# Two heads with both kinds of attention in one item, row tiles in pairs, and normalisation after attention

## The reference

```
q, k, v = heads(x @ qkv_w + qkv_b)
std_logits = (q . k) / 4                              # "dot", 16 numbers a head
write = exterior(x_prev @ w1_write, x @ w2_write)     # 6 numbers a head, unit length
read  = exterior(x @ w1_read,  x @ w2_read)
geo_logits = (read . (write @ J6)) * inc_scale        # "geometric", 6 numbers a head
std_out = softmax(causal(std_logits)) @ v
geo_out = softmax(causal(geo_logits)) @ (x @ geo_w + geo_b)
gate = mean over heads of sigmoid(x @ gate_w + gate_b)
x = layernorm(x + ((1-gate)*std_out + gate*geo_out) @ out_w + out_b)
x = layernorm(x + (silu(x @ wg.T) * (x @ wu.T)) @ wd.T)    # 768 hidden columns
```

## Time and profile before

| | us |
|---|---|
| median of 3 runs | 2109.17 (2107.64 to 2111.22) |
| the profiled execution, span | 2112.1 |
| PE busy | 1930.6 (91%) |
| ACT busy | 1273.4 (60%) |
| DVE busy | 1129.4 (53%) |
| POOL busy | 336.9 (16%) |

### The profile page before, as it was taken

One profiled execution on the slowest core, in us unless ns is written; L12 is line 12 of the kernel. 1 busy time (PEld: TensorE's weight loads), 2 busy tenths in 40 slices (PEclk: granted clock), 3 DMA queues, 4 the chain that ended last, 5 costly groups with the idle time before them and its releaser, 6 DMA issues. The chain is left out here.

```text
span 2112.1 us, 35917 instructions
## 1 busy us (share of the span) xinstructions
PE 1930.6 (91%) x11400; PEld 769.0 (36%) x11400; DVE 1129.4 (53%) x2179; ACT 1273.4 (60%) x1641; POOL 336.9 (16%) x609
## 2 busy tenths in 40 slices
PE   8888498999998999999899999989999995899998
PEld 4444122333332333333233333323333322556555
DVE  5666377565564655556465655646565403443442
ACT  4555544577776777677677767767777783222121
POOL 3333303111211110111111011111101111000000
PEclk9999699999999999999999999999999997999999
DMA  6668660404133250414324041432500004112000
GB/s 192 205 211 254 163 107 25 86 21 90 37 70 46 50 86 6 91 20 73 49 47 86 6 91 21 72 46 50 86 6 30 4 11 103 43 51 65 20 20 20
DMA packets 138525, 145.83 MB, mean 69 GB/s; under 512 B 46784, under 2 KB 120768, under 8 KB 136288
## 3 DMA queue, kind: packets, MB, share of 16 engines
q1 hardware_dynamic: 137136, 140.32, 30.4%
q0 software_dynamic: 624, 2.75, 0.4%
q10 hardware_dynamic: 576, 0.28, 0.1%
HBM read 88.25 MB, written 54.53 MB: 68 GB/s over the span
## 5 line engine op out<-in xcount | busy, mean ns | idle before, releaser
L931 ACT ACTIVATE prob<-ex 128x1024 f32<-128x1024 f32 (+2 forms) x1280 | 1074.5, 893 | 444.4 <-PE ex L776 438.8
L946 DVE TENSOR_REDUCE mp<-mx 128x1 f32<-128x512 f32 (+3 forms) x1280 | 749.2, 609 | 547.4 <-PE mx L794 287.5
L776 PE MATMUL ex<-qa,ka 98*128 98x512 bf16 (+3 forms) x2560 | 675.6, 354 | 62.7 <-issue 28.3
L827 PE MATMUL pv<-prob,va 128*32 128x512 f32 (+3 forms) x5120 | 613.4, 552 | 7.6 <-POOL prob L752 7.3
L791 PE MATMUL mx<-ka,qa 96*128 96x512 bf16 (+3 forms) x1280 | 450.1, 353 | 14.7 <-DVE mp L946 13.8
L752 POOL TENSOR_SCALAR_AFFINE_SELECT prob<-prob 128x256 f32<-128x256 f32 x512 | 205.8, 408 | 1288.3 <-ACT prob L931 1287.8
L776 PEld LDWEIGHTS ex<-qa,ka 98*128 98x128 bf16 x2560 | 200.2, 99 | 474.3 <-ACT prob L931 306.3
L791 PEld LDWEIGHTS mx<-ka,qa 96*128 96x128 bf16 x1280 | 123.7, 97 | 340.4 <-DVE mp L946 239.1
L827 PEld LDWEIGHTS pv<-prob,va 128*32 128x32 f32 x5120 | 101.7, 108 | 206.7 <-issue 181.8
L1291 ACT ACTIVATE sg<-pg 128x512 f32<-128x512 f32 x48 | 28.7, 597 | 185.6 <-PE pg L1213 185.5
L794 PE MATMUL mx<-mask_qk,ident 128*128 128x128 bf16 x512 | 113.1, 221 | 0.0
(11 more groups left out here) (101 smaller groups left out, 964.7 us busy)
## 6 DMA issues: line engine op xcount, KB each, us to landing
parts<-sp SPq DMA_DIRECT2D x64, 384.0 KB, 3.3
qa<-parts SPq DMA_DIRECT2D x192, 128.0 KB, 6.7
ka<-parts SPq DMA_DIRECT2D x192, 128.0 KB, 8.6
values<-vn SPq DMA_DIRECT2D x64, 256.0 KB, 3.3
va<-values SPq DMA_DIRECT2D x16, 1024.0 KB, 13.8
heads<-on SPq DMA_DIRECT2D x64, 128.0 KB, 1.9
att<-heads SPq DMA_DIRECT2D x64, 128.0 KB, 3.0
xc<-in_xt SPq DMA_DIRECT2D x8, 513.0 KB, 4.2
```

Source lines behind the costliest of these rows:

```text
L776: last = pe.matmul(dst, ka[which][0:NROWM, h, kb * P:(kb + 1) * P], qa[which][0:NROWM, h, (qt + 1) * CH - w:(qt + 1) * CH], start=True, st ...
L827: last = pe.matmul(pv[h * VW:(h + 1) * VW, qt % 2, CH - w:CH], va[kind][:, kb, h * VW:(h + 1) * VW], prob[(s * HG + h) % 8][:, at[j]:at[j] ...
L931: act.activation(prob[n % 8][:, 0:w], ex[:, n % 2, 0:w], ACT.Exp).then_inc(ex_done, 1)
L946: v.tensor_reduce(out=mp[kind][:, h * NKB + qb, k0 // CH:k0 // CH + 1], in_=mx[:, u % 2, 0:w], axis=AX.X, op=ALU.max).then_inc(mx_free[kin ...
```

## The change

An item now holds two heads with both kinds (16 items again, each a batch and a pair of heads). Four streams are in it: geometric and dot of head 0 and head 1.

- Scores: the geometric ones of the two heads stand in rows 0 to 37 and 64 to 101 of one operand, as two row tiles of 64x128 (six products of 6 rows and two rows for the maxima). The dot ones take 98 rows for the first head and 128 for the second, one after the other. One exponential covers one kind of both heads and one key block of 512 or 384 columns.
- Maxima of the dot scores come in pairs of row tiles too (`max_pair`, K = 64: four of the six products), into a ring of three banks. The mask is added by DVE while it reduces. All items have them, 80 tiles for the next item; 80 stand in a prologue ahead of item 0. The branch over the geometric maxima stands in every item.
- The V product has its four column tiles for the four streams, one bank, and stands between the geometric and the dot scores of a key block. V is padded with ones, so the denominators come out on 16 rows. `turn` and the division go; the products are stored as they are (`raw`).
- Row maxima are written by eight DMAs an item instead of two. There are three operand sets, loaded two items ahead.
- `project` makes six packed rows a chunk instead of eight: the lines have 6 numbers a head and no padding.
- `finish` loads values and denominators (9 DMAs, 2.5 MB a chunk), DVE inverts the denominators (`inverse`), POOL multiplies (`weigh`, four operations), DVE adds the two kinds (`mixed`). The transposes of the mix go, as the stored products already stand turned. The gates are worked out in the last item of attention.

```diff
-HG = 4
+PAIRS_OF_HEADS = H // 2
+ITEMS = B * PAIRS_OF_HEADS
+MX_RING = 3
...
+                        if kind == GEO:
+                            rows = slice(HALF * a, HALF * a + GEO_FULL)
+                            lhs, rhs = k_set[rows, kb * P:(kb + 1) * P], q_set[rows, (qt + 1) * CH - w:(qt + 1) * CH]
+                        else:
+                            rows = slice(0, DOT_FULL[a])
...
+            def max_pair(nxt, u):
...
+                for a in range(2):
+                    t = 2 * u + a
+                    if t >= MX_RING:
+
+                        pe.wait_ge(mx_free, nit * NTILE + t + 1 - MX_RING)
+                    rows = slice(HALF * a, HALF * a + DOT_MAIN)
+                    pe.matmul(mx[:, t % MX_RING, 0:w], q_set[rows, a, qb * P:(qb + 1) * P],
+                              k_set[rows, a, k0:k0 + w], start=True, stop=True).then_inc(mx_ready, 1)
...
+                for j in range(groups):
+                    scores(it, which, s, j, GEO, head)
+                    some(j)
+                    earlier(j)
+                    scores(it, which, s, j, DOT, head)
+                    if j == groups - 1:
+                        some(groups)
+                    if j == 0 and s == MT_STEP and nxt:
+                        max_rows(nxt)
...
+                for a in range(2):
+                    for i in range(2):
...
+                            q.dma_start(dst.rearrange("p (k t) -> p k t", t=P),
+                                        mrow[n:n + NKB, i, :]).then_inc(m_in, 16)
...
+            def inverse(c, par):
+
+                v.wait_ge(att_in[par], (c // 2 + 1) * 9 * 16)
+                v.sem_inc(v_passed, 1)
+                v.reciprocal(den[par][:, :, :, :], den[par][:, :, :, :]).then_inc(inv_ready, 1)
...
                     if m == 2 and has_mix:
-                        mixed(c + 2, par, False)
+                        inverse(c + 2, par)
...
+                if has_mix:
+                    mixed(c + 2, par, False)
                 add_up(c, par, SECOND, not has_second)
```

More of the change, by code:

```diff
@@ new lines, in step, with earlier @@
+            def step(at, before, nxt, s, head):
+                it, which, use = at
+                places = shares(s) if nxt else [[] for _ in range(1 + len(STEPS[s][1]))]
+                groups = len(STEPS[s][1])
+                def some(i):
+                    for u in places[i]:
+                        max_pair(nxt, u)
+                def earlier(j):
+                    prev, ps = (at, s - 1) if s else (before, NSTEP - 1)
+                    if prev is not None and j < len(STEPS[ps][1]):
+                        times_v(*prev, ps, j, head)
+                for j in range(groups):
[7 more added lines that the diff above has]
+                        max_rows(nxt)
+                for j in range(groups, 2):
+                    earlier(j)
@@ new lines, in item @@
+            def item(at, before, nxt, head):
+                it, which, use = at
+                pe.wait_ge(sets[which]["geo_in"], (use + 1) * LOADS * 16)
+                pe.wait_ge(m_in, (it + 1) * 128)
+                for s in range(NSTEP):
+                    step(at, before, nxt, s, head)
+                    if s == 3 and isinstance(it, int) and it == LAST_ITEM:
+                        pe.wait_ge(gate_ready, 4)
+                        pe.transpose(mx[0:NC * TT, 0, 0:P], gate[:, :], ident[:, :]).then_inc(gate_turned, 1)
@@ L921, in _ @@
+            for it in range(ITEMS - 3, ITEMS):
+                item(static(it), static(it - 1), static(it + 1) if it < LAST_ITEM else None, False)
+            times_v(*static(LAST_ITEM), NSTEP - 1, 0, False)
         @block.scalar
@@ L1026, in _, with finish @@
+            for u in range(NMT):
+                max_pair(0, u)
+            max_rows(0, True)
+            item(0, True, True)
+            with v.Fori(1, ITEMS - 1) as it:
+                item(it, False, True)
+            item(ITEMS - 1, False, False)
             take(ITEMS - 1, NQT - 1, False)
-            normalise(ITEMS - 1, NQT - 1, False)
-def finish(nc, x, heads, gate_z, ident, weights, out):
+def finish(nc, x, raw, gates, ident, weights, out):
     NT = NC * TT
@@ L1438, with by_pair @@
     qkv_w, qkv_b = a["attn_qkv_w"], a["attn_qkv_b"]
+    def by_pair(geo, dot):
+        both = [v.reshape(v.shape[:-1] + (PAIRS_OF_HEADS, 2 * DH)) for v in (geo, dot)]
+        return np.stack(both, -2).reshape(geo.shape[:-1] + (2 * D,))
     laid = {
```

971 lines of the change are left out of this document (492 added, 479 removed).

## The result

| | before | forecast | after |
|---|---|---|---|
| median of the runs, us | 2109.08 (2107.64 to 2111.22) | 2036 | 2489.96 (2486.89 to 2496.95) |
| span of the profiled execution, us | 2112.1 | 2039 | 2485.2 |
| first scores at, us | 250.71 | 288 | 340.17 |
| end of attention at, us | 1763.4 | 1586 | 2027.66 |
| output layers, us | 348.7 | 453 | 457.5 |

The changed kernel is slower: ratio 1.181 (95% interval 1.179 to 1.183). The forecast missed the sign, and the time lies outside the range. Of the 446.2 us by which the span misses the forecast, 52.2 come from the start (340.17 against 288), 389.5 from attention (1687.5 against 1298), 4.5 from the output layers.

A forecast was written before the change was run, and what follows sets the result against it. PE was taken to set attention's pace. Attention ending at 1586 (first scores 288, 15 items of 82, a last of 66) plus output layers 453 gave 2039, on the runs' scale 2036 us, 3.5% faster; range 1945 to 2165.

The forecast's parts named there:

- the end of an item: Attention, between items: PE waits about 3 us for eight row DMAs; with branch and clock 7.2 (5.3 to 8.1); nothing else late.
- rival of a lower clock in attention: Attention: gaps every few us lower the granted clock, 0.97 before; over 2150 us, chance 0.04.
- The start: Projections 25 us shorter (10 to 40), then memsets 11.5, prologue 49, rows 10: first scores at 288 against 250.71.
- PE's stream: PE in attention: row tiles run at once, third tile-shape change 0.09 each; 70.5 us an item.
- rival of pairs one by one: Attention on PE: row tiles don't run at once, 14.8 us more an item, 2265 us; chance 0.14.
- part case of 0.28 a pair: Attention on PE: row-tile pairs at 0.28 in place of 0.22 us, adding 69, 2105 us; chance 0.06.
- The masked reduction: DVE in attention: adding the mask while reducing costs the plain 0.61 us, over 32 of 80 tiles an item.
- rival of a doubled price: DVE in attention: masked reduction at twice the price, prologue 14 us longer, PE waiting 5 more an item: 2125; chance 0.13.
- The item: Attention: 70.5 stream, 3.5 ring, 7.2 end of item, 0.6 bank exchange make 82 us an item (77 to 90).
- the ring: Attention: three banks of maxima make PE wait about one tile's 0.5 us in seven steps, 3.5 an item.
- The skipped branch: Ends of items: the branch over exact geometric maxima, now in every item, idles PE 0.75 to 2.3 us.
- The output layers: Head 25 us more, six rounds 13.5 more each (10.6; 16.6 if DVE and POOL take turns), transposes 2 less: 453.

The follow-up runs named there:

- e1: The changed kernel with each operand load issued as two DMAs, one a slot, rows outermost: 2198.65 us, 1.043 to the kernel before.
- e4: The changed kernel with four buffers instead of two for the V products on their way out, nothing else: 2182.98 us, 1.035 to the kernel before.
- e5: The changed kernel with loads by rows, stores as two DMAs of 64 rows, and four output buffers together: 2136.71 us, 1.015 to the kernel before.
- e6: e5 with the transpose of the maxima and the eight row DMAs one step earlier: 2131.82 us, 1.012 to the kernel before.
- e7: e5 with a chunk's reciprocal in six pieces, the mix behind the third sum, POOL's products started per kind: 2077.63 us, 0.985 to the kernel before.

## Why the prediction was wrong, step by step

**The step that failed** is the sentence on the end of an item: the eight row DMAs stand on SP ahead of the 24 loads and the store, and "those have a whole item until needed (three operand sets), so nothing else is late". That holds for the loads, not for the store: its buffer is one of two, and DVE's next copy but one needs it. It put the delay at nothing. What the runs showed in its place is a wait of some 22 us in 13 of the items, 291.4 us of DVE, and 298.0 of PE behind it. And the loads got no price at all, though the diff turns their outermost dimension from 16 rows to 2 slots. No row of before shows a load of the new shape, and the sentence gave it neither a lower nor an upper bound. With rows outermost in the loads (e1) or the wait taken out (e4) 291 and 307 us of the miss go, and with both and the store by rows (e5) 351 of the span. None of the rivals named this: they looked at PE and DVE, and the DMA queue was treated as an order without a rate. The rival of a lower clock in attention names what went with the stall: 0.87 in the kernel after is 0.95 in e5.

**The start.** A chunk's chain on DVE did get shorter, 22.6 us from one to the next (101.02 to 123.65) in place of 27.36, more than the 3.0 charged. What the sum left out is SP's queue here too. Operands are now loaded two items ahead, so the 24 loads of the second item stand in the projections, and they are slow. First, ACT waits 30.7 us in all for stores that stand among the loads of the first item, so its last operation there ends only 2.8 earlier than before (233.1 against 235.9). Second, the last chunk's stores stand behind the 24 loads of the second item, which are issued from 219.06 on:

```profile
252.74 12.62 SPq L337 DMA_DIRECT2D parts_dot<-sp  x4
```

Attention begins when they have landed; until then ACT is idle for 41.2 us (the line of ACT L982 above), where it was 5.8 before. So attention's first operation on ACT came 32.7 us later than before in place of 25 earlier. In e5 ACT's last operation ends 24.1 earlier than before, as forecast, though as a larger gain less 9.2 of such waits; but it is idle for 18.2 behind it, since the loads stand ahead of the last stores there too, and attention starts 11.7 earlier. That lies near the lower bound of 10, by luck: the bound was set for ACT and the gates, not for SP. Memsets took 11.9 (11.5 charged). The prologue to the transpose took 46.4 (286.24 to 332.64; charged 49), and the rows 7.5 (charged 10).

**PE's stream.** The row tiles do run at once, and this term was right. PE in mid-item, kernel after, answers to the earlier trace rows:

```profile
1041.48 1.06 PE L902 MATMUL pv<-prob,va 128*32 128x512 f32 x8
1042.48 0.61 PE L836 MATMUL ex<-dq,dk 98*128 98x512 bf16 x2
1043.07 0.39 PE L836 MATMUL ex<-gq,gk 38*128 38x512 bf16 x2
1043.30 0.38 PE L857 MATMUL mx<-dk,dq 64*128 64x512 bf16 x2
1043.61 1.06 PE L902 MATMUL pv<-prob,va 128*32 128x512 f32 x8
1044.61 0.61 PE L836 MATMUL ex<-dq,dk 98*128 98x512 bf16 x2
1045.15 0.39 PE L836 MATMUL ex<-gq,gk 38*128 38x512 bf16 x2
```

A pair of 512 columns starts 0.23 before what follows (1043.07 to 1043.30), as a single whole-array matmul did. Two dot matmuls take 0.54 to 0.59 until the next pair, 0.44 by themselves: 0.10 to 0.15 for the third change of tile shape (charged 0.09). From one V block to the next it is 2.13 (1041.48 to 1043.61), as forecast (2.1). The rival of pairs one by one, and the part case of 0.28 a pair, fell.

**The masked reduction** has the plain price. The groups by line, kernel after (busy us, mean ns, idle before):

```profile
L1010 DVE TENSOR_REDUCE mp<-mx 128x1 f32<-128x512 f32 x768 | 490.7, 685 | 294.2 <-PE mx L857 294.0
L1006 DVE CUSTOM_DVE_ANT_0 dull<-mx,mask_qk 128x128 f32<-128x128 f32 (+3 forms) x512 | 234.1, 489 | 304.6 <-PE mx L857 300.6 <-issue 3.3
...
L1006 DVE DVE_READ_ACCUMULATOR2_ANT mp<- 128x1 f32 x512 | 42.7, 83 | 0.0
```

And one of 512 columns in order of time:

```profile
1003.38 0.69 DVE L1006 CUSTOM_DVE_ANT_0 dull<-mx,mask_qk 128x512 f32<-128x512 f32 x1
```

It takes 0.69 where the plain one takes 0.64 to 0.65, with 0.08 behind it for the result; the rival of a doubled price fell.

**The item.** In the kernel after the first and the last of fifteen items, without the wait for the store, take 86.5 us, the others 109 to 113.6. In e5 they take 84.1 to 89.1, mean 87.0, against 82 (77 to 90): right in kind, 5 short. In the one e5 item at full clock (984.29 to 1068.43, 84.1) PE is busy 73.9 where 70.5 were counted. The waits in e5's fifteen items, prologue left out, are 3.0 each for ACT's exponentials (45.4; charged 0.6), 3.1 for the rows (37.1, and 8.7 at three ends of items that the view names issue and that are gone in e6; charged 3) and 1.3 for the ring (19.3; charged 3.5). With 73.9 that is 81.3; the rest of the 84.1 is in smaller waits, 0.9 of it for POOL's masks. The other 3 of the 87 go with the clock (0.94 in an item of e5 from 816 to 900 us, 1.00 in the one above): a stretch at the lower level follows 14 of e5's 15 ends of items. The first matmul behind the rows at one end of an item, kernel after:

```profile
1089.14 0.61 PE L836 MATMUL ex<-gq,gk 38*128 38x512 bf16 x2 [3.70 <-DMA dq<-mrow]
```

The window of the 12 us that it opens, with the columns of the table by stage:

```profile
1089.00:1101.00 12.00, 10.58 (x55) 2.74 (x56) 4.34 (x17) 5.18 (x6) 2.57 (x6) 0.50 0.10 36
```

At 0.50, the level of 1.2 GHz, some 5 us of PE's time are lost in one item (half of 10.58), where at most 3 were charged. The skipped branch, charged 0.75 to 2.3 in every item, shows no gap of its own in twelve of e6's fifteen; the three with 2.9 are those of the loop's jump.

**The output layers** came out at 457.5 against 453, with two errors that partly cancel: the head took 76.5 (69 charged), and the rounds 51.5 in place of 38.7, so +12.8 (+13.5 charged). DVE's order of time in one round, kernel after, answers to the earlier trace rows:

```profile
2216.10 12.94 DVE L1382 RECIPROCAL den<-den 128x2048 f32<-128x2048 f32 x1
2228.96 0.63 DVE L1460 SCALAR_TENSOR_TENSOR ht<-pg,sg 128x512 f32<-128x512 f32 x1
2229.50 9.40 DVE L1450 TENSOR_SCALAR res<-sums,mean_var,rstd 128x256 f32<-128x256 f32 x4
```

POOL's there:

```profile
2229.22 2.35 POOL L1244 TENSOR_TENSOR den<-den,gb 128x1024 f32<-128x1024 f32 x1 [39.79 <-DVE den L1382]
...
2236.41 2.34 POOL L1248 TENSOR_TENSOR att<-att,den 128x1024 f32<-128x1024 f32 x1
```

PE's, the hidden block that awaits the fourth ht and the down product that awaits the last one:

```profile
2229.64 3.78 PE L1301 MATMUL pg<-y_t,wg_f 128*128 128x512 f32 x4 [7.95 <-DVE ht L1460]
...
2240.24 10.62 PE L1317 MATMUL po<-wd_f,ht 128*128 128x256 f32 x48 [3.21 <-DVE ht L1460]
```

The reciprocal takes the 12.95 worked out. DVE's four scalings last 9.40 beside POOL's four products in place of 1.38 without them (2213.82): 2.35 each, the length of one product. So they take turns, as the upper bound had it, but of the 6 that the bound gave them only 2.6 reach PE: it waits 3.21 ahead of the down product in place of 0.62. The reciprocal costs it 7.95 ahead of the hidden block (8.4 charged) and 2.9 by the lower clock behind that gap (the block's two groups of matmuls take 3.58 and 2.77 to the next start in place of 1.72 each; 2 charged). With 0.9 less for the mix's transposes that is 12.6 of the 12.8. The 13.5 lay midway between turns and no turns, and that 2.9 for turns fits the 2.6 is luck.

**The budget.** From e5's span (2134.4) to the forecast's (2039) 95 us remain: 8 in the first scores, 75 in fifteen items, 8 in the last one, 4 in the output layers. So with the DMAs and the buffers put right the time lies within the range, but the forecast was 5% low (2136.71 against 2036) and had the sign wrong even so: 1.5% slower in place of 3.5% faster, most of it in the items.

## What to carry to other kernels

Where a diff changes the shape of a DMA, compare its outermost dimension with the one before, not only its KB, and price the queue in time: what is issued behind it, and whose buffer that frees. A store behind prefetches can be on the critical path when its buffers are few: here there were two for four stores an item, and with four the wait was gone. And one long operation can cost another engine its whole length if it stands ahead of what that engine needs: with the reciprocal in pieces that fit the idle gaps, and POOL's products moved with them, 59 us came back (e5 to e7).

## What was not expected of the hardware

A DMA whose outermost dimension is 2 used 2.05 of 16 engines (54 GB/s), and cutting it in two along the inner dimension left 2.1 engines. Against 16 busy engines (132 GB/s) the rate fell by a factor of 2.4, not of 8. Not only the load is slow: a store of 256 KB issued behind such loads landed 18 us later, and one of 64 rows a DMA still kept DVE waiting up to 20.6. A gap of 3.7 us on PE was followed by 12 us at a granted clock of 0.50 with PE 88% busy, while one of 3.04 in e5 (991.89) was followed by full clock, and one of 2.78 there (466.98) again by a fall (0.57 over the next 12 us). So the length of the gap alone doesn't decide it; what does, no run here shows.
